# First attention: shared values weighed for two heads at a time, in three fp32r passes, with weight splits moved behind the own result

## The chip, the cores and the metric

One core of a Trainium2 chip runs the whole program. The metric is the device time of one execution in microseconds; lower is better. Five engines work side by side, each on its own instruction list in order, and wait for one another by semaphores: TensorE (PE in the profile, its weight loads PEld), VectorE (DVE), ScalarE (ACT), GpSimd (POOL), and SyncE (SP), which here issues DMAs.

## The reference

Two transformer layers of attention and feed-forward, with layer norms between; x is 4 x 256 tokens of 512. The change lies in the first attention only:

```python
q = (x @ w_q) ...            # 32 heads of 128
k = (x @ w_k) ...            # 8 heads
v = (x @ w_v) ...            # 8 heads, each shared by 4 query heads
lq = x @ w_lq                # 128 wide
lk = (lq @ w_lk) ...         # 32 heads of its own
lv = (x @ w_lv) ...          # 32 heads of its own
q, k, lk = rope(q), rope(k), rope(lk)
attn = causal_attn(q, repeat(k, 4), repeat(v, 4))
lat  = causal_attn(q, lk, lv)
return attn @ w_o + lat @ w_lo
```

So every query head is used twice: with the key and value shared by its group of four ("shared"), and with its own latent key and value ("own").

## The kernel before, in words

The first attention runs over 8 groups g of four heads (one shared key and value each). A group has 16 heads steps, 4 batches of 256 tokens by 4 heads h. A step s carries three heads at different stages, so the code speaks of `st` (this step), `before` (the step before, `st.near(-1)`) and `st.near(-2)`. The loop runs s from 2 to 17 in each group; h is s modulo 4, so steps 4, 8, 12 and 16 have h = 0. The steps at 16 and 17 already belong to the next group's first batch where there is one.

TensorE in a step (`a0_tensor_step`, L1074): `turn(0)`, three transposes of the normalised shared probabilities of `before` into bank PT; `scores()` of this head against shared and own keys, into banks 2 and 3; at h = 2 the keys of the next batch; `weigh(0)`, probabilities times shared values, into the first half of bank OB; `turn(1)` and later `weigh(1)`, the same for the own ones; the projection of the queries two steps ahead; `output(0)` and `output(1)`, the results of the head before the last times w_o and w_lo, added up in two banks over a batch; at h = 0 the values of the batch (`a0_values`). In step 16 TensorE waits, right before the values, for the weight chunks 6 to 10 (`weights(pe, st, range(C_LVV, C_WO))`).

Precision: nearly all products are made of fp32r parts. An operand is held as a high part (rounded by a ScalarE copy) and a low part (VectorE or GpSimd subtracts), and `product()` (L363 in the trace) makes three passes, high-high, high-low and low-high. Weighing and transposing were plain f32; there one matmul call shows as two MATMUL instructions in the trace.

ScalarE in a step (`a0_scalar_step`, L1210): copy of the turned shared probabilities (`turned_out(0)`, L1224), high part of the rotated queries (L1208), four exponentials (L1217), at h = 2 the key's swap, `result_hi(0)` (L1229), `turned_out(1)`, high parts of this step's weight chunks (L259), at h = 2 the key's high part, swap of the queries' halves (L1202, L1203), `result_hi(1)`.

VectorE (`a0_vector_step`, L1322): the rotation's sum of the queries (`a0_rotate`, L1319), minima of the scores (L1331, L1333), inverse sums, at h = 2 the key's sum, `result_lo(0)` (L1346), low parts of the weight chunks (L265), the cosine product (`a0_cosine`, L1310), `result_lo(1)`, at h = 1 the two additions to x (L1388), at h = 0 the values out of PSUM (L1353), and late splits. GpSimd does the sine product (L1417), the low part of the rotated queries (L1425) and the normalisation (L1436, L1438).

A group's weights are 19 chunks of 128 x 512: 0 keys, 1 to 4 queries, 5 latent keys, 6 to 10 values, 11 to 14 w_o, 15 to 18 w_lo. `SPLIT_AT` says in which step which chunks are split into W, `WEIGHTS_FOR` in which step TensorE waits for which. SyncE loads them into four raw buffers, each again as soon as its low part has been made.

## Time and profile before

| what | us |
|---|---|
| median of 3 runs | 1802.55 (1802.38 to 1802.89) |
| the profiled execution | 1804.75 |
| its span, first to last instruction | 1802.9 |
| TensorE busy | 1742.7 |
| VectorE, ScalarE, GpSimd busy | 1095.0, 1083.6, 931.1 |

Busy time counts any moment in which an engine has an instruction running. The span is what the views of the trace measure; what lies around it belongs to the launch. Ends of matmuls are modelled, so for TensorE the chain of work, which counts each matmul from the end of the one before, is the better measure of pace.

### The profile page before, as it was taken

What the parts mean: (1) busy time and instruction counts of PE and PEld (TensorE: products, weight loads), DVE (VectorE), ACT (ScalarE), POOL (GpSimd) and SP (SyncE); (2) the same over time, 40 slices, a digit from 0 to 9 for tenths busy, and PEclk for the clock granted to TensorE, in tenths of its full rate; (3) what the DMA queues carried; (4) which work ended last, traced back from release to release, by engine and by line L of the source; (5) the groups of instructions that cost most, each with busy time, mean ns of one, the idle gap of its engine ahead of it and who ended that gap; (6) DMA issues with size and microseconds to landing.
All of it is one profiled execution on the core that took longest, in us unless ns stands there. A gap on an engine that the chain in (4) does not pass through costs nothing.

```text
span 1802.9 us, 32176 instructions
## 1 busy us (share of the span) xinstructions
PE 1742.7 (97%) x11116; PEld 1520.7 (84%) x11116; DVE 1095.0 (61%) x3305; ACT 1083.6 (60%) x3077; POOL 931.1 (52%) x1170
## 2 busy tenths in 40 slices
PE   7999999999999999999999999999999998899798
PEld 6789999999999998999899899989888776677567
DVE  6675465556456546645654664565566677788756
ACT  3355566567556656655765664566563264788864
POOL 4555545455544555554555554455542255777850
PEclk9999999999999999999999999999999999999999
DMA  4300021012002101200110120020012121000101
GB/s 145 109 27 7 18 60 36 1 43 64 7 18 59 36 1 48 65 1 19 59 36 1 49 64 1 19 75 21 1 59 59 42 60 46 2 2 2 37 12 47
DMA packets 35424, 65.79 MB, mean 36 GB/s; under 512 B 4032, under 2 KB 4672, under 8 KB 35264
## 3 DMA queue, kind: packets, MB, share of 16 engines
q1 hardware_dynamic: 35264, 63.73, 11.7%
q8 instruction: 91, 1.49, 0.3%
q14 instruction: 69, 0.57, 0.1%
HBM read 61.62 MB, written 2.10 MB: 35 GB/s over the span
## 4 chain that ended last, share of the span: by engine, by line
PE 76%; DVE 8%; ACT 8%; issue 5%; POOL 3%; DMA 0%; SPq 0%; DVEq 0%; POOLq 0%; ACTq 0%
PE bank L363 58%; PE bank L1105 6%; PE bank L1092 4%; PE bank L1107 3%; ACT s L1217 2%; PE bank L1672 2%; PE bank L1643 1%; ACT s L1738 1%; DVE h L761 1%; PE bank L1659 1%; DVE work L772 1%; POOL h L839 1%; DVE work L1319 1%; ACT h L684 1%; POOL rstd L328 1%
## 5 line engine op out<-in xcount | busy, mean ns | idle before, releaser
L363 PE MATMUL bank<-W,oT 128*128 128x512 f32 x1632 | 432.2, 400 | 0.6 <-DVE x L1875 0.6
L1425 POOL TENSOR_TENSOR qk<-work,qk 128x512 fp32r<-128x512 f32 (+1 forms) x160 | 193.9, 1212 | 427.0 <-ACT qk L1208 427.0
L363 PEld LDWEIGHTS bank<-W,oT 128*128 128x128 f32 x1632 | 288.3, 189 | 48.5 <-DVE x L1875 1.1
L1224 ACT COPY pt<-bank 128x384 f32<-128x384 f32 x256 | 122.0, 477 | 324.0 <-PE bank L1092 323.3
L1417 POOL TENSOR_TENSOR work<-work,table 128x512 f32<-128x512 f32 (+1 forms) x160 | 190.8, 1192 | 132.8 <-ACT work L1203 132.8
L1217 ACT ACTIVATE s<-s,neg_max 128x128 f32<-128x128 f32 (+1 forms) x512 | 227.5, 445 | 49.1 <-DVE neg_max L1333 48.1
L363 PE MATMUL bank<-W,xnA 128*128 128x320 f32 (+1 forms) x1056 | 191.0, 335 | 2.3 <-DVE xnA L348 1.7
L1310 DVE TENSOR_TENSOR work<-bank,table 128x512 f32<-128x512 f32 (+1 forms) x160 | 102.1, 638 | 130.0 <-ACT work L1203 129.9
L363 PEld LDWEIGHTS bank<-W,xnA 128*128 128x128 f32 x1056 | 166.3, 189 | 15.2 <-DVE xnA L348 2.6
L1438 POOL TENSOR_TENSOR s<-s,inv_sum 128x256 f32<-128x256 f32 x256 | 168.2, 657 | 0.0
L363 PE MATMUL bank<-qk 128*128 128x256 f32 (+1 forms) x768 | 165.9, 351 | 0.9 <-POOL qk L1425 0.9
L1353 DVE COPY lvv<-bank 128x320 f32<-128x320 f32 x128 | 62.9, 491 | 169.6 <-PE bank L363 169.1
L363 PE MATMUL bank<-xnB,W 128*128 128x256 f32 (+1 forms) x1080 | 161.7, 299 | 0.9 <-DVE xnB L348 0.9
L1105 PE MATMUL bank<-pt,lvv 128*128 128x256 f32 x512 | 153.9, 382 | 8.9 <-DVE oT L1346 8.2
L363 PE MATMUL bank<-xnA,W 128*128 128x256 f32 (+1 forms) x1080 | 161.2, 299 | 0.6 <-DVEq L1264 0.3
L363 PEld LDWEIGHTS bank<-xnB,W 128*128 128x128 f32 x1080 | 143.2, 191 | 7.2 <-DVE xnB L348 1.3
L363 PEld LDWEIGHTS bank<-xnA,W 128*128 128x128 f32 x1080 | 143.1, 190 | 7.3 <-DVE work L1310 0.7
L1208 ACT CAST qk<-work 128x512 fp32r<-128x512 f32 (+1 forms) x160 | 92.4, 577 | 83.2 <-DVE work L1319 83.0
L1989 POOL TENSOR_TENSOR s<-s,b_inv_sum 128x384 f32<-128x384 f32 x128 | 114.1, 913 | 51.9 <-DVE b_inv_sum L1897 51.4
L265 DVE TENSOR_TENSOR W<-raw,W 128x512 fp32r<-128x512 f32 x148 | 108.2, 768 | 30.3 <-ACT W L259 30.1
L1436 POOL TENSOR_TENSOR s<-s,inv_sum 128x128 f32<-128x128 f32 x256 | 104.1, 407 | 42.0 <-DVE inv_sum L1341 42.0
L1092 PE MATMUL bank<-table,s 128*128 128x128 f32 x768 | 125.5, 272 | 0.0
(111 smaller groups left out, 3501.8 us busy)
## 6 DMA issues: line engine op xcount, KB each, us to landing
raw<-in_weights SPq DMA_DIRECT2D x215, 256.0 KB, 2.7
x<-in_x SPq DMA_DIRECT2D x8, 256.0 KB, 5.4
out<-x SPq DMA_DIRECT2D x8, 256.0 KB, 2.1
row<-in_bias_rows SPq DMA_DIRECT2D x5, 256.0 KB, 2.7
table<-in_constants SPq DMA_DIRECT2D x4, 240.0 KB, 3.1
b_qk<-in_bias_rows SPq DMA_DIRECT2D x1, 512.0 KB, 3.5
b_val<-in_bias_rows SPq DMA_DIRECT2D x1, 256.0 KB, 3.0
table<-in_constants SPq DMA_DIRECT2D x1, 66.0 KB, 2.4
```

What stands on the lines that cost most here:

```text
L265: nc.vector.tensor_tensor(dst[LO], raw[:, s, :], dst[HI].bitcast(F32), ALU.subtract).then_inc(w_split, 1)
L363: last = nc.tensor.matmul(out_ap, lhs(i), rhs(j), start=start and k == 0, stop=stop and k == 2)
L1092: last = nc.tensor.transpose(bank[PT][:, blk * P:(blk + 1) * P], s0[:, s, blk * P:(blk + 1) * P], ident)
L1105: nc.tensor.matmul(bank[OB][:, 0:SEQ], lvv[:, 0, col:col + P], pt0[:, k, 0:2 * P], start=True, stop=False)
L1217: last = nc.scalar.activation(s0[:, s, cols], s0[:, s, cols], ACT.Exp, bias=neg_max[:, s, qt:qt + 1], scale=-1.0, accum_out=row_sum[:, s, ...
L1224: nc.scalar.copy(pt0[:, k, :], bank[PT][:, 0:3 * P]).then_inc(a_pt, 1)
L1310: nc.vector.tensor_tensor(work[:, 2 + s, cols], bank[fs][:, cols], table[:, T_COS + cols.start:T_COS + cols.stop], ALU.mult).then_inc(a_pr ...
L1417: nc.gpsimd.tensor_tensor(work[:, s, cols], work[:, s, cols], table[:, T_SIN + cols.start:T_SIN + cols.stop], ALU.mult).then_inc(a_sin, 1)
L1425: nc.gpsimd.tensor_tensor(lo, work[:, 2 + s, st.columns(what)], hi.bitcast(F32), ALU.subtract).then_inc(a_rope_lo, 1)
L1436: nc.gpsimd.tensor_tensor(s0[:, s, 0:P], s0[:, s, 0:P], inv_sum[:, s, 0:1].to_broadcast([P, P]), ALU.mult)
L1438: nc.gpsimd.tensor_tensor(s0[:, s, P:3 * P], s0[:, s, P:3 * P], inv_sum[:, s, 1:2].to_broadcast([P, 2 * P]), ALU.mult).then_inc(a_norm, 1)
L1989: nc.gpsimd.tensor_tensor(blocks, blocks, b_inv_sum[:, at, 1:4].unsqueeze(2).to_broadcast([P, 3, P]), ALU.mult).then_inc(b_norm, 1)
```

## The change

The shared values get a high and a low part of their own (`vs`), and so do the turned shared probabilities (`pt_pair`, two heads side by side). ScalarE makes the high part of the probabilities as the first thing in a step (`turned_hi`), VectorE the low part as its first, ahead of the rotation's sum (`turned_lo`). In every even step `weigh_pair` weighs two heads' shared probabilities at once, in three fp32r passes, into the whole bank OB; its result is taken out by `pair_hi` and `pair_lo` on 512 columns. The own half stays f32, once a step (`weigh_own`). Both still share bank OB, and both turns bank PT: `turn(1)` now waits for the low part. `output(0)` comes one or two steps later than before: none at h = 2, one at h = 0 and h = 3, two at h = 1. ScalarE and VectorE make the parts of the weight chunks after the own result's part. Chunk 13 is split in step 3, chunk 12 in step 17; `WEIGHTS_FOR` follows.

```diff
 
-SPLIT_AT = {2: [17, 14], 3: [18], 11: [1], 12: [0, 2], 13: [3, 6], 14: [4, 7], 15: [8, 9],
-            16: [10, 11, 15, 12], 17: [16, 13]}
+SPLIT_AT = {2: [17, 14], 3: [18, 13], 11: [1], 12: [0, 2], 13: [3, 6], 14: [4, 7], 15: [8, 9],
+            16: [10, 11, 15], 17: [16, 12]}
 SPLIT_LATE = {13: [5]}
 SPLIT_FROM = 11
 TURN = [c for s in sorted(SPLIT_AT) for c in SPLIT_AT[s] + SPLIT_LATE.get(s, [])]
 OWN = sum(len(c) for s, c in SPLIT_AT.items() if s < SPLIT_FROM)
 BEFORE = TURN[OWN:]
 
-WEIGHTS_FOR = {2 + h: [C_WO + h, C_WLO + h] for h in range(GH)}
+WEIGHTS_FOR = {2: [C_WLO], 3: [C_WO, C_WLO + 1], 4: [C_WO + 1, C_WLO + 2],
+               5: [C_WO + 2, C_WO + 3, C_WLO + 3]}
 WEIGHTS_FOR.update({14: [C_K, C_Q], 15: [C_Q + 1], 16: [C_Q + 2], 17: [C_Q + 3]})
...
-                lvv = sb(s, "lvv", [P, 2, LVW])
-                pt0 = sb(s, "pt0", [P, 2, 3 * P])
-                oT0 = [sb(s, f"oT0_{i}", [P, 4, SEQ], F32R) for i in (HI, LO)]
+                lvv = sb(s, "lvv", [P, 2, GH * HD])
+                vs = [sb(s, f"vs{i}", [P, 2, HD], F32R) for i in (HI, LO)]
+                pt_pair = [sb(s, f"pt_pair{i}", [P, 2, 3, P], F32R) for i in (HI, LO)]
+                pt_own = sb(s, "pt_own", [P, 3 * P])
+                o_pair = [sb(s, f"o_pair{i}", [P, 2, SEQ], F32R) for i in (HI, LO)]
+                o_own = [sb(s, f"o_own{i}", [P, 2, SEQ], F32R) for i in (HI, LO)]
                 lqT = [sb(s, f"lqT{i}", [P, TOKENS], F32R) for i in (HI, LO)]
...
+            before = st.near(-1)
+
             def turn(k):
-                n, s = st.near(-1).inst(k)
+                n, s = before.inst(k)
                 pe.wait_ge(a_norm, n + 1)
-                pe.wait_ge(a_pt, n + 1)
+                if k == 0:
+                    pe.wait_ge(a_pt_own, before.number() + 1)
+                else:
+                    pe.wait_ge(a_pt_lo, before.number() + 1)
                 for blk in range(3):
                     last = nc.tensor.transpose(bank[PT][:, blk * P:(blk + 1) * P],
                                                s0[:, s, blk * P:(blk + 1) * P], ident)
                 last.then_inc(a_turned, 1)
 
-            def weigh(k):
-                before = st.near(-1)
-                n, _ = before.inst(k)
-                col = before.h * P if k else GH * P
-                if before.h == 0 and k == 0:
+            def weigh_pair():
+                pe.wait_ge(a_pt_lo, before.number() + 1)
+                pe.wait_ge(a_own_lo, before.number() + 1)
+                to = bank[OB][:, :].rearrange("p (e q) -> p e q", e=2)
+                product(to, lambda p: vs[p][:, 0, :],
+                        lambda p: pt_pair[p][:, :, 0:2, :].rearrange("p e b q -> p e (b q)"), True, False)
+                product(to[:, :, P:SEQ], lambda p: vs[p][:, 1, :],
+                        lambda p: pt_pair[p][:, :, 2, :], False, True).then_inc(a_pv_pair, 1)
+
+            def weigh_own():
+                col = before.h * P
+                if before.h == 0:
                     pe.wait_ge(a_proj_free, before.fill(3)[0] + 3)
-                pe.wait_ge(a_pt, n + 2)
-                pe.wait_ge(a_o_lo, n + 1)
-
-                nc.tensor.matmul(bank[OB][:, 0:SEQ], lvv[:, 0, col:col + P], pt0[:, k, 0:2 * P],
+                pe.wait_ge(a_pt_own, before.number() + 2)
+                if before.paired():
+                    pe.wait_ge(a_pair_lo, before.pair() + 1)
+                else:
+                    pe.wait_ge(a_own_lo, before.number() + 1)
+
+                nc.tensor.matmul(bank[OB][:, 0:SEQ], lvv[:, 0, col:col + P], pt_own[:, 0:2 * P],
                                  start=True, stop=False)
-                nc.tensor.matmul(bank[OB][:, P:SEQ], lvv[:, 1, col:col + P], pt0[:, k, 2 * P:3 * P],
-                                 start=False, stop=True).then_inc(a_pv, 1)
-
-            def output(k):
-                done = st.near(-2)
-                n, s = done.inst(k)
-                first, end = done.h == 0 and k == 0, done.h == GH - 1 and k == 1
+                nc.tensor.matmul(bank[OB][:, P:SEQ], lvv[:, 1, col:col + P], pt_own[:, 2 * P:3 * P],
+                                 start=False, stop=True).then_inc(a_pv_own, 1)
+
+            def output(k, done):
+                first, end = done.h == 0 and k == 1, done.h == GH - 1 and k == 1
                 if first:
                     pe.wait_ge(a_added, done.added)
                 if first and done.number() == 0:
                     pe.wait_ge(a_lq_lo, 2)
-                pe.wait_ge(a_o_lo, n + 2)
...
+                if k:
+                    pe.wait_ge(a_own_lo, done.number() + 2)
+                    of, slot = o_own, done.number() % 2
+                else:
+                    pe.wait_ge(a_pair_lo, done.pair() + 1)
+                    of, slot = o_pair, done.h % 2
                 w = ((C_WLO if k else C_WO) + done.h) * CH
                 for tt in range(2):
-                    last = product(bank[OUTB[tt]][:, :], lambda p: oT0[p][:, s, tt * P:(tt + 1) * P],
...
-            if lag1:
-                weigh(0)
+            if lag2 and st.h == 0:
+                output(0, st.near(-3))
+            if lag1 and before.paired():
+                weigh_pair()
                 turn(1)
             if st.queries and not st.first:
                 a0_queries(pe, st)
+            if lag1 and not before.paired():
+                turn(1)
...
-            if lag2:
-                output(0)
+            if lag2 and st.h in (1, 3):
+                output(0, st.near(-3))
+            if lag2 and st.h == 1:
+                output(0, st.near(-2))
+            if lag2 and st.h != 1:
+                output(1, st.near(-2))
             if lag1:
-                weigh(1)
-            if lag2:
-                output(1)
+                weigh_own()
+            if lag2 and st.h == 1:
+                output(1, st.near(-2))
             if st.h == 0 and st.heads:
                 if st.s == STEPS0:
                     weights(pe, st, range(C_LVV, C_WO))
...
             turn_of = None if st.last_group else st.g
             if lagging(st):
-                turned_out(0)
+                turned_hi()
             if before.queries:
                 a0_rope_hi(act, before, "q")
             if st.heads:
@@ -1239,19 +1295,20 @@
                 a0_swap(act, st, "k")
             if st.heads:
                 exponentials(1)
+            if lagging(st) and before.paired():
+                pair_hi()
             if lagging(st):
-                result_hi(0)
-                turned_out(1)
+                turned_own()
             if st.last_group and st.s == STEPS0:
                 first_use(ACT.Silu)
-            for stream, j, dst in step_splits(st, False):
-                stream.split_hi(act, j, dst, turn_of)
             if st.key:
                 a0_rope_hi(act, st, "k")
             if st.queries and not st.first:
                 a0_swap(act, st, "q")
             if lagging(st):
-                result_hi(1)
+                own_hi()
+            for stream, j, dst in step_splits(st, False):
+                stream.split_hi(act, j, dst, turn_of)
             for stream, j, dst in step_splits(st, True):
                 stream.split_hi(act, j, dst, turn_of)
             for t in next_norms(st):
...
+            def turned_lo():
+                dve.wait_ge(a_pt_hi, before.number() + 1)
+                hi, lo = [pt_pair[i][:, before.h % 2, :, :].rearrange("p b q -> p (b q)") for i in (HI, LO)]
+                nc.vector.tensor_tensor(lo, bank[PT][:, 0:3 * P], hi.bitcast(F32),
+                                        ALU.subtract).then_inc(a_pt_lo, 1)
+
+            def pair_lo():
+                dve.wait_ge(a_pair_hi, before.pair() + 1)
+                hi, lo = [o_pair[i][:, :, :].rearrange("p e q -> p (e q)") for i in (HI, LO)]
+                nc.vector.tensor_tensor(lo, bank[OB][:, :], hi.bitcast(F32),
+                                        ALU.subtract).then_inc(a_pair_lo, 1)
+
+            def own_lo():
+                dve.wait_ge(a_own_hi, before.number() + 1)
+                hi, lo = [o_own[i][:, before.number() % 2, :] for i in (HI, LO)]
+                nc.vector.tensor_tensor(lo, bank[OB][:, 0:SEQ], hi.bitcast(F32),
+                                        ALU.subtract).then_inc(a_own_lo, 1)
 
             def values(i):
                 tt, half = divmod(i, 2)
                 f, fs = st.fill(i)
                 dve.wait_ge(a_proj, f + 1)
-                nc.vector.tensor_copy(lvv[:, tt, half * HALF:(half + 1) * HALF],
-                                      bank[fs][:, 0:HALF]).then_inc(a_proj_free, 1)
+                if half == 0:
+                    nc.vector.tensor_copy(lvv[:, tt, 0:HALF], bank[fs][:, 0:HALF]).then_inc(a_proj_free, 1)
+                    return
+                own = GH * HD - HALF
+                shared = bank[fs][:, own:HALF]
+                nc.vector.tensor_copy(vs[HI][:, tt, :], shared).then_inc(a_v_hi, 1)
+                nc.vector.tensor_copy(lvv[:, tt, HALF:GH * HD], bank[fs][:, 0:own])
+                dve.wait_ge(a_v_hi, st.values_before() + tt + 1)
+                nc.vector.tensor_tensor(vs[LO][:, tt, :], shared, vs[HI][:, tt, :].bitcast(F32),
+                                        ALU.subtract).then_inc(a_proj_free, 1)
             turn_of = None if st.last_group else st.g
+            if lagging(st):
+                turned_lo()
             if before.queries:
                 a0_rotate(dve, before, "q")
             if st.heads:
@@ -1372,14 +1451,14 @@
                 ln_apply(dve, 16 + t, t % 2, x[:, t, :], normed[:, t, :])
             if st.key:
                 a0_rotate(dve, st, "k")
-            if lagging(st):
-                result_lo(0)
-            for stream, j, dst in step_splits(st, False):
-                stream.split_lo(dve, j, dst, turn_of)
+            if lagging(st) and before.paired():
+                pair_lo()
             if st.queries and not st.first:
                 a0_cosine(dve, st, "q")
             if lagging(st):
-                result_lo(1)
+                own_lo()
+            for stream, j, dst in step_splits(st, False):
+                stream.split_lo(dve, j, dst, turn_of)
             if st.h == 1 and not st.second:
                 done = st.near(-2)
                 for tt in range(2):
```

## Rows read from the trace of the kernel before

**Rows 1.** The page's busy line.

```profile
PE 1742.7 (97%) x11116; PEld 1520.7 (84%) x11116; DVE 1095.0 (61%) x3305; ACT 1083.6 (60%) x3077; POOL 931.1 (52%) x1170
```

**Rows 2.** Busy by window, from:to, length, engines, TensorE's granted clock, DMA.

```profile
230.00:250.00 20.00, 19.02 (x122) 16.88 (x121) 14.51 (x39) 14.32 (x39) 10.95 (x14) 1.00 0.20 58
1000.00:1200.00 200.00, 199.02 (x1266) 181.46 (x1265) 114.18 (x354) 126.27 (x356) 101.82 (x135) 1.00 0.13 38
```

**Rows 3.** The chain over a plain batch: start, length, what.

```profile
504.58 0.33 PE bank L1092 x3
504.91 1.06 PE bank L363 x6
505.97 0.43 PE bank L1105 x2
506.40 0.22 PE bank L1107 x2
...
506.95 3.18 PE bank L363 x21
...
510.79 1.39 PE bank L363 x6
...
512.51 2.48 PE bank L363 x18
...
535.00 8.42 PE bank L363 x54
543.42 0.33 PE bank L1092 x3
```

**Rows 4.** The chain, start of step 13 in the first and last group.

```profile
230.65 0.33 PE bank L1092 x3
...
1325.90 0.33 PE bank L1092 x3
```

**Rows 5.** Waits, 200 to 1280 us: total us, times, longest.

```profile
PE bank L1105 <- DVE oT L1346: 3.5, 7, 1.0
...
PEld bank L1105 <- ACT pt L1224: 9.5, 17, 1.4
```

**Rows 6.** The chain in steps 14 to 16.

```profile
558.23 0.67 PE bank L1105 x2
...
566.03 0.67 PE bank L1105 x2
...
574.51 8.42 PE bank L363 x54
```

**Rows 7.** ScalarE's timeline, steps 13 to 16: start, length of the instructions together.

```profile
550.70 0.62 ACT L259 CAST W<-raw 128x512 fp32r<-128x512 f32 x1
...
557.12 0.35 ACT L1229 CAST oT<-bank 128x256 fp32r<-128x256 f32 x1
557.37 0.48 ACT L1224 COPY pt<-bank 128x384 f32<-128x384 f32 x1
557.74 1.15 ACT L259 CAST W<-raw 128x512 fp32r<-128x512 f32 x2
...
559.22 0.58 ACT L1202 COPY work<-bank 64x512 f32<-64x512 f32 x1
...
565.34 0.47 ACT L1224 COPY pt<-bank 128x384 f32<-128x384 f32 x1
...
573.12 2.18 ACT L259 CAST W<-raw 128x512 fp32r<-128x512 f32 x4
```

**Rows 8.** VectorE's timeline, steps 13 and 14.

```profile
551.38 1.27 DVE L1388 TENSOR_TENSOR x<-x,bank 128x512 f32<-128x512 f32 x2
552.57 0.69 DVE L265 TENSOR_TENSOR W<-raw,W 128x512 fp32r<-128x512 f32 x1
553.17 0.69 DVE L1319 TENSOR_TENSOR work<-work 128x512 f32<-128x512 f32 x1
...
557.67 0.42 DVE L1346 TENSOR_TENSOR oT<-bank,oT 128x256 fp32r<-128x256 f32 x1
```

More of the change, by code:

```diff
@@ L901, in program @@
         a_turned = sem("a_turned")
-        a_pt = sem("a_pt")
-        a_pv = sem("a_pv")
-        a_o_hi = sem("a_o_hi")
-        a_o_lo = sem("a_o_lo")
+        a_v_hi = sem("a_v_hi")
+        a_pt_own = sem("a_pt_own")
+        a_pt_hi = sem("a_pt_hi")
+        a_pt_lo = sem("a_pt_lo")
+        a_pv_own = sem("a_pv_own")
+        a_pv_pair = sem("a_pv_pair")
+        a_own_hi = sem("a_own_hi")
+        a_own_lo = sem("a_own_lo")
+        a_pair_hi = sem("a_pair_hi")
+        a_pair_lo = sem("a_pair_lo")
         a_out = sem("a_out")
@@ L934, in near, with values_before, paired, pair @@
                 return Step(self.g, self.s + d)
+            def values_before(self):
+                return 2 * (self.g * BATCH + self.batch)
+            def paired(self):
+                return self.s % 2 == 1
+            def pair(self):
+                return self.number() // 2
             def number(self):
@@ L1117, in output @@
                     pe.wait_ge(a_lq_lo, 2)
-                pe.wait_ge(a_o_lo, n + 2)
+                if k:
[4 more added lines that the diff above has]
+                    of, slot = o_pair, done.h % 2
                 w = ((C_WLO if k else C_WO) + done.h) * CH
                 for tt in range(2):
-                    last = product(bank[OUTB[tt]][:, :], lambda p: oT0[p][:, s, tt * P:(tt + 1) * P],
+                    last = product(bank[OUTB[tt]][:, :], lambda p: of[p][:, slot, tt * P:(tt + 1) * P],
                                    lambda p: W[p][:, w:w + CH], first, end)
@@ L1260, in a0_vector @@
         def a0_vector(dve):
-            for s, n in ((a_proj_free, 2), (a_rope_lo, 2), (a_min, 2), (a_pt, 1), (a_o_lo, 1),
-                         (a_added, 1)):
+            for s, n in ((a_proj_free, 2), (a_rope_lo, 2), (a_min, 2), (a_pt_own, 1),
+                         (a_own_lo, 1), (a_added, 1)):
                 dve.sem_inc(s, n)
```

26 lines of the change are left out of this document (14 added, 12 removed).

## The prediction, made before the result was known

> **What bounds the kernel.** I read the busy line of the page first [rows 1]: TensorE is busy for 97% of the span, the others for 52 to 61%. Over 200 us in the middle of the first attention it is 99.5%, at full clock [rows 2]. So there TensorE's own order is the time, and what it saves comes back unless it then waits for somebody. The chain of work that ended last gives the true pace (it counts a matmul from the end of the one before), and a step can be added up from it [rows 3]: a turn (three transposes) 0.33 us; scores 1.06; one head's weighing 0.43 + 0.22 = 0.65; queries with one output 3.18, of which the output is 1.39, so queries 1.79; keys 2.48 - 1.06 = 1.42; values 8.42 - 1.39 = 7.03. A batch of four steps runs from 504.58 to 543.42, 38.84 us. Step 13 (numbers within a group) begins at 230.65 in the first group and at 1325.90 in the last [rows 4]: seven groups took 1095.25 us, where 28 plain batches would be 1087.5. So 7.7 us, 1.1 a group, are stalls. The table of waits says at what: at the weighing, for ScalarE's copy of the probabilities or for VectorE's low part [rows 5], and the chain shows them in steps 14 and 15, behind weight splits: pieces of 0.67 where 0.43 is usual [rows 6].
>
> **Gain on TensorE.** A pair of heads cost four weighings of 0.65 us. The two with own values stay. The two with the shared value head (1.30) become one product of three fp32r matmuls on 512 columns and three on 256. The scores have exactly these six, in strips of 256 and 128 columns: 1.06 us [rows 3]; elsewhere in the chain the same x6 piece reads 1.04 and 1.05. I take 1.05. Saved: 0.25 us a pair, 64 pairs, 16.0 us; 15 to 17 by the spread of the six. The outputs only move between steps, eight a batch as before. The steps' own lengths become 8.33 us (h=1, three outputs), 8.02 (h=2, one), 6.94 (h=3), 15.02 (h=0).
>
> The Trainium skill, "VectorE: DVE Perf Modes", section on the TRN2 errata, lists a matmul at max(60, 6 + columns) cycles, whatever its type. By it a head's f32 weighing of four instructions would be 0.33 us and the new product 0.98, so this edit would cost 0.32 us a pair, 20 us, instead of saving 16. The trace has 0.43 us for two f32 instructions of 256 columns [rows 3], where the rule gives 0.22, so the trace does not agree, and the row is taken.
>
> **Loss one: the values wait for chunk 10.** In step 16 (h=0) TensorE waits, just ahead of the values, for chunks 6 to 10, and chunk 10 is split in this very step. Before, ScalarE started those splits at 573.12 [rows 7], behind the copy of the probabilities, and the values began at 575.9 (574.51 plus an output) without a wait [rows 6]. Now the splits stand behind the own result, which exists only after the own weighing, TensorE's last instruction ahead of the values. Counted from its end: 0.03 to the result's copy, 0.25 until ScalarE can start the next (557.12 to 557.37), 0.62 for the split [rows 7], 0.03, 0.69 on VectorE, 0.38 until the matmul runs (VectorE's result ended at 558.09 [rows 8]; the weighing stretched by 0.24 from 558.23 ran as if from 558.47 [rows 6]). That is 2.0 us, with nothing to hide it, in seven groups (the last has no values to come): 14.0 us. Bounds: with no handover to TensorE 1.6 each, 11 us; with 0.2 more on VectorE and in the handovers 2.2 each, 15.4 us.
>
> **Loss two: VectorE comes late to the next step.** Call d the time from a step's start until VectorE takes up its first instruction, now the low part of the probabilities. On 384 columns, between 0.42 at 256 and 0.69 at 512 [rows 8], it takes 0.56, with 0.47 until the next starts. Queued behind it: the rotation's sum, so its high part on ScalarE, the minima, the exponentials, the own copy. In step 14 before, the sum started at 553.17 and the exponentials were done at 557.12, 3.95 later, keys between [rows 7, 8]. Now ScalarE's pair result follows (512 columns, 0.6 by its other casts of that size) and VectorE's low part of it (0.69). The own weighing shares their bank, so in an h=2 step it can go at d + 0.47 + 3.95 + 0.60 + 0.03 + 0.69 + 0.38 = d + 6.12; TensorE is there at 7.37. The pair's product can go at d + 0.56 + 0.42; TensorE is there at 2.81 (h=2) or 2.78 (h=0). In an h=3 step, with no keys (exponentials 0.9 earlier) and no pair, the own copy ends at d + 4.0 and is used 0.46 later (565.81 to 566.27 [rows 6, 7]); TensorE is there at 6.29.
>
> Without splits d is 0.8 to 0.95, and all of these hold, by 0.3 us or more: no stall. With them:
> Step 13 has two splits, the additions to x and a late split, now all behind the own result. From its start: weighing over at 6.95, VectorE's low part to 7.76, two low splits to 9.07, additions 1.19, late split 0.60 [rows 8]: 10.86, so d = 2.55 for step 14. Before it was 553.17 less 551.02 (543.42 plus 7.60), 2.15. Step 14 then stalls 0.72 at the pair and 0.62 more at the own weighing: 1.34, and lasts 9.36. ScalarE in it: own copy to 7.83, keys' high part to 8.2, swap of the queries 1.17 to 9.4 (two of [rows 7]'s 0.58), own result, two splits to 10.8; VectorE behind it to 11.6. So d = 2.25 in step 15: 0.42 at the own weighing. Its two splits leave d = 2.15 in step 16: 0.36 at the pair. Steps 17, 2 and 3 have two splits each too (3 had one before): d = 1.97 in step 2 gives 0.14 + 0.62, then 0.42 in step 3 and 0.36 in step 4. Sum 2.12 + 1.54 = 3.66 a group where 1.1 was, 2.56 more, in seven groups 17.9 us. In the last group steps 14 to 16 have no queries, so ScalarE and VectorE alone set them, and the new low parts lengthen their chain by 0.5 to 1 us each: 2 us. Bounds: with each of the six places 0.3 us milder, 5 us; 0.2 worse, 28 us. A gain is not excluded: the queries' cosine now comes ahead of the splits; if that healed the old stalls too, -7.7.
>
> **Hidden.** The shared values' high and low parts (three instructions in place of one copy of 320 columns) add 0.4 us on VectorE per half of tokens. TensorE fills a bank of values in 1.76 us, a quarter of 7.03, so this lies beside the values; only the last reaches into an h=1 step (d = 0.95), which has over 1 us to spare. Uncovered it would be 0.4 a batch, 13 us. ScalarE's pair copy replaces two of half its size. Chunks 12 and 13 are still split a step or more ahead of their outputs. Four raw buffers reload in about 3 us against a step's 7.
>
> **Sum.** -16.0 + 14.0 + 17.9 + 2 = +17.9 us. The profiled execution took 1804.75 us (its span 1802.9, and 1.85 around it), so it would be 1822.7; against the median of 1802.55, which is 2.2 lower, 1820.
>
> **Rivals.**
> A. Only chunk 10 counts; the slips are no worse than the old stalls. -16 + 14 = -2: 1800.5, within 0.2% (3.6 us, about what a measurement of this kernel can tell from no change). For it: the cosine no longer waits for splits. Against: VectorE was the releaser in step 14 even with d = 2.15, and now has more in front.
> B. The other side, faster: neither loss, only the shorter product. 1786.5; with half of loss one 1794. It is decided at one point: whether chunk 10's low part is ready within 0.6 us of the own weighing's end. For it: the pair's product is earlier than the old two weighings together. Against: own copy, split and low split cannot start before that weighing ends, and they are 1.3 us of work alone.
> C. The idle of 2 us costs TensorE its clock: values at 1.2 GHz, 7 us more in seven groups, 49 us: 1869. Against: between 230 and 250 us it idled 1 us in all, at clock 1.00 [rows 2]; no row shows 2 us in one piece. The Trainium skill, "TensorE: Matmul & The Clock Gate", section "Why this matters for your kernels", warns of idle gaps between bursts; the rows bear out only that shorter ones do no harm.
> D. The slips feed on each other: 5.5 us a group in place of 3.66, because steps 2 and 3 shrink and now have four splits. 1833.
>
> **Chances.** The forecast 0.60, D 0.12, C 0.03, A 0.13, B 0.12. So slower 0.75, same 0.12, faster 0.13. The likeliest is 1820, its own range 1808 to 1830; the range for 8 in 10 takes in A and half of B: 1794 to 1832.
>
> **What will show it.** Right: six-matmul pieces of about 1.05 us twice a batch in the chain and half as many f32 weighings; TensorE waits 2 us ahead of the values of every fourth batch, released by VectorE's split; steps 14 to 16 and 2 to 4 stall at the pair's product or the own weighing, behind VectorE or ScalarE. Wrong: values that begin without a wait, a d in step 14 of 2.15 or less, or plain batches that stall too. Their margin in h=2 is 0.3 us; if it is gone, 16 more steps pay, and it would be slower still.

## The result, and the profile after

The changed kernel takes 1842.48 us (1838.84 to 1844.56, four runs), the kernel before in the same session 1802.72: a ratio of 1.0214, 95% interval 1.0194 to 1.0235. It is slower, as forecast, but by 39.8 us where 17.5 were forecast, and outside the range of 1794 to 1832.

The page of the changed kernel, its busy line; TensorE is as busy as before, over a span 38.5 us longer (1841.4 against 1802.9):

```profile
PE 1743.9 (95%) x10988; PEld 1508.9 (82%) x10988; DVE 1159.0 (63%) x3498; ACT 1072.4 (58%) x3013; POOL 913.0 (50%) x1169
```

The chain of work that ended last, changed kernel, through steps 13 to 16 (start, length, what; step 17 starts at 595.64). L367 is `product()`, L1118 the turns, L1141 and L1143 the own weighing:

```profile
545.43 7.04 PE bank L367 x48
552.46 0.33 PE bank L1118 x3
552.79 2.84 PE bank L367 x21
555.63 0.33 PE bank L1118 x3
555.96 2.77 PE bank L367 x12
558.73 0.43 PE bank L1141 x2
559.16 0.23 PE bank L1143 x2
...
559.42 0.37 ACT o_own L1285
559.79 0.53 ACT W L263
...
560.35 1.29 DVE W L269 x2
561.64 0.16 DVE x L1467
...
588.33 7.31 PE bank L367 x48
595.64 0.33 PE bank L1118 x3
```

A batch without splits is TensorE's throughout. Here the chain leaves TensorE at the own result in step 13 and stays with ScalarE and VectorE for 21.7 us (559.42 to 581.12), until the pair's product of step 16. Before, it did so too in these steps, but for 13.2 us (544.86 to 558.10), until the weighing in step 14. From the start of step 13 (552.46) to that of step 17 (595.64) there are 43.18 us; a batch without splits lasts 38.22 (the values end at 514.25 and 552.46, a batch apart), where it was 38.84 [rows 3]. So a plain batch gains 0.62 us, and these four steps lose 4.96.

TensorE's timeline there; the brackets give its idle time and who ended it:

```profile
563.96 1.33 PE L367 MATMUL bank<-pt_pair,vs 128*128 128x512 f32 x6 [0.39 <-DVE pt_pair L1403]
...
569.63 0.67 PE L1141 MATMUL bank<-pt_own,lvv 128*128 128x256 f32 x2 [0.83 <-DVE o_pair L1409]
...
581.16 1.31 PE L367 MATMUL bank<-pt_pair,vs 128*128 128x512 f32 x6 [0.50 <-DVE pt_pair L1403]
...
588.33 1.88 PE L367 MATMUL bank<-W,xnA 128*128 128x320 f32 x11 [1.71 <-DVE W L269]
```

The forecast places are there: the pair's product in step 14, the own weighing in 14, the pair's product in 16, the values in 16; in step 15 the own weighing (576.97) runs 0.70 us instead of 0.59. The table of waits between 200 and 1300 us counts them over the groups (before: [rows 5]):

```profile
PE bank L367 <- DVE W L269: 11.9, 7, 1.7
PE bank L1141 <- DVE o_pair L1409: 11.7, 14, 0.8
PE bank L367 <- DVE pt_pair L1403: 10.1, 21, 0.5
```

Seven waits for chunk 10, 1.7 us each; with the slower start of the values behind (7.31 in place of 7.04) 1.96 each.

The whole difference, from starts of the same step in the two chains: step 5 of the first group comes 2.5 us later (155.55 against 153.07). From there seven groups take 1121.73 us against 1093.33, 28.4 more, or 160.25 against 156.19 a group. From step 5 of the last group to the layer norm's statistics that follow it in the chain (1399.16 against 1358.33) it is 121.9 us against 111.9, 10.0 more. After that the changed kernel is 2.3 us quicker. Sum 38.6.

The 2.5 us of the start hold slips of steps 2 to 4 (with fewer splits there, in e9, step 5 comes at 151.67) and a slow stretch of TensorE: behind an idle of 2.46 us (116.26 to 118.72) its granted clock was 0.52 between 120 and 122 us, and twelve output matmuls took 4.35 us in the chain where the kernel before took 2.76 at clock 1.00.

### The profile page after: what moved, and what is told of

Same layout as the page of the kernel before. It is cut to its first block, busy times and chain, and to the rows that moved or that the text cites. A ratio compares the mean times of both kernels' runs of the same rounds, so it can differ in the third digit from the quotient of the medians.

```text
span 1841.4 us, 32013 instructions
## 1 busy us (share of the span) xinstructions
PE 1743.9 (95%) x10988; PEld 1508.9 (82%) x10988; DVE 1159.0 (63%) x3498; ACT 1072.4 (58%) x3013; POOL 913.0 (50%) x1169
## 4 chain that ended last, share of the span: by engine, by line
PE 63%; DVE 13%; ACT 12%; issue 8%; POOL 3%; DMA 0%; DVEq 0%; SPq 0%; POOLq 0%; ACTq 0%
PE bank L367 51%; PE bank L1118 3%; DVE W L269 3%; ACT s L1264 3%; PE bank L1141 2%; DVE work L1376 2%; PE bank L1751 2%; ACT s L1817 1%; ACT work L1250 1%; ACT work L1249 1%; PE bank L1722 1%; DVE work L1367 1%; DVE pt_pair L1403 1%; DVE h L765 1%; PE bank L1143 1%
## 5 line engine op out<-in xcount | busy, mean ns | idle before, releaser
L1504 POOL TENSOR_TENSOR qk<-work,qk 128x512 fp32r<-128x512 f32 (+1 forms) x160 | 188.4, 1178 | 583.6 <-ACT qk L1255 583.5
L367 PE MATMUL bank<-W,xnA 128*128 128x320 f32 (+1 forms) x1056 | 193.0, 337 | 14.7 <-DVE W L269 11.9
L367 PE MATMUL bank<-W,o_own 128*128 128x512 f32 x768 | 202.4, 399 | 0.0
L1271 ACT CAST pt_pair<-bank 128x384 fp32r<-128x384 f32 x128 | 61.5, 480 | 238.1 <-PE bank L1118 238.1
L367 PE MATMUL bank<-W,o_pair 128*128 128x512 f32 x768 | 198.8, 401 | 0.0
L367 PEld LDWEIGHTS bank<-W,xnA 128*128 128x128 f32 x1056 | 165.5, 189 | 27.8 <-DVE W L269 13.3
L367 PE MATMUL bank<-qk 128*128 128x256 f32 (+1 forms) x768 | 166.0, 352 | 0.9 <-POOL qk L1504 0.9
L367 PEld LDWEIGHTS bank<-W,o_pair 128*128 128x128 f32 x768 | 140.2, 189 | 27.4
L367 PE MATMUL bank<-xnB,W 128*128 128x256 f32 (+1 forms) x1080 | 160.2, 298 | 0.8 <-DVE xnB L352 0.8
L1517 POOL TENSOR_TENSOR s<-s,inv_sum 128x256 f32<-128x256 f32 x256 | 160.4, 627 | 0.0
L367 PEld LDWEIGHTS bank<-W,o_own 128*128 128x128 f32 x768 | 139.5, 191 | 25.2
L367 PE MATMUL bank<-xnA,W 128*128 128x256 f32 (+1 forms) x1080 | 158.5, 297 | 0.6 <-DVEq L1321 0.3
L367 PEld LDWEIGHTS bank<-xnB,W 128*128 128x128 f32 x1080 | 146.4, 191 | 10.5 <-DVE xnB L352 1.3
L367 PEld LDWEIGHTS bank<-xnA,W 128*128 128x128 f32 x1080 | 145.4, 190 | 10.0 <-DVE work L1367 0.7
L1118 PE MATMUL bank<-table,s 128*128 128x128 f32 x768 | 126.6, 274 | 2.7 <-DVE pt_pair L1403 2.7
L1398 DVE RECIPROCAL inv_sum<-row_sum 128x2 f32<-128x2 f32 x256 | 42.1, 165 | 132.3 <-ACT s L1264 132.3
L367 PE MATMUL bank<-W,xnB 128*128 128x320 f32 x768 | 116.5, 311 | 0.0
```

What stands on the lines that cost most here:

```text
L367: last = nc.tensor.matmul(out_ap, lhs(i), rhs(j), start=start and k == 0, stop=stop and k == 2)
L1118: last = nc.tensor.transpose(bank[PT][:, blk * P:(blk + 1) * P], s0[:, s, blk * P:(blk + 1) * P], ident)
L1271: nc.scalar.copy(pt_pair[HI][:, before.h % 2, :, :].rearrange("p b q -> p (b q)"), bank[PT][:, 0:3 * P]).then_inc(a_pt_hi, 1)
L1398: nc.vector.reciprocal(inv_sum[:, s, :], row_sum[:, s, :]).then_inc(a_inv, 1)
L1504: nc.gpsimd.tensor_tensor(lo, work[:, 2 + s, st.columns(what)], hi.bitcast(F32), ALU.subtract).then_inc(a_rope_lo, 1)
L1517: nc.gpsimd.tensor_tensor(s0[:, s, P:3 * P], s0[:, s, P:3 * P], inv_sum[:, s, 1:2].to_broadcast([P, 2 * P]), ALU.mult).then_inc(a_norm, 1)
```

## Experiments

Each is compared with the kernel before in the same session, which took 1803.9 to 1805.4 us there. "Group" is the mean time from step 5 of one group to step 5 of the next, over seven groups. "Early" and "late" say where a step splits its weight chunks: ahead of the own result, as before, or behind it, as in the change.

| kernel | us | ratio, 95% interval | group, us |
|---|---|---|---|
| before | 1802.7 | 1 | 156.19 |
| changed | 1842.5 | 1.0214 (1.0194 to 1.0235) | 160.25 |
| e1 changed, splits early | 1791.7 | 0.9927 (0.9911 to 0.9944) | 154.42 |
| e2 changed, early in step 16 only | 1833.6 | 1.0159 (1.0144 to 1.0175) | 158.67 |
| e3 changed, sum ahead of low part | 1853.9 | 1.0276 (1.0260 to 1.0291) | 161.67 |
| e5 before, splits late | 1819.0 | 1.0081 (1.0066 to 1.0096) | 158.10 |
| e4 as e1, sum ahead of low part | 1810.4 | 1.0027 (1.0016 to 1.0038) | 156.70 |
| e6 changed, no low part | 1809.0 | 1.0027 (1.0016 to 1.0038) | 156.99 |
| e7 changed, ScalarE early, VectorE late | 1900.1 | 1.0523 (1.0507 to 1.0538) | 167.83 |
| e8 as e1, splits spread | 1791.8 | 0.9923 (0.9908 to 0.9938) | 154.28 |
| e9 changed, splits spread | 1835.5 | 1.0167 (1.0150 to 1.0184) | 159.25 |
| e10 before, late, one VectorE instruction more | 1851.4 | 1.0258 (1.0243 to 1.0274) | 161.99 |
| e11 before, one VectorE instruction more | 1828.7 | 1.0138 (1.0123 to 1.0153) | 158.93 |
| e12 changed, old step lengths | 1866.5 | 1.0353 (1.0337 to 1.0368) | 164.10 |
| e13 as e1, old step lengths | 1835.3 | 1.0178 (1.0161 to 1.0195) | 160.17 |

### e1: the splits back at their old place

First ScalarE's step, then VectorE's:

```diff
             if st.last_group and st.s == STEPS0:
                 first_use(ACT.Silu)
+            for stream, j, dst in step_splits(st, False):
+                stream.split_hi(act, j, dst, turn_of)
...
             if lagging(st):
                 own_hi()
-            for stream, j, dst in step_splits(st, False):
-                stream.split_hi(act, j, dst, turn_of)
...
             if lagging(st) and before.paired():
                 pair_lo()
+            for stream, j, dst in step_splits(st, False):
+                stream.split_lo(dve, j, dst, turn_of)
...
             if lagging(st):
                 own_lo()
-            for stream, j, dst in step_splits(st, False):
-                stream.split_lo(dve, j, dst, turn_of)
```

> The changed kernel with the weight splits back at their old place on both engines (ScalarE behind the own probabilities' copy, VectorE behind the pair's low part); all else as changed. Theory S, the loss is the splits' place: the wait for chunk 10 (2.0 us a group, 14 us) goes, and most of the slips in steps 14 to 16 and 2 to 4 (5.3 us a group now): 1792 to 1802 us. Rival L, the loss is the longer chain of the pair itself (a low part at the head of VectorE's queue, a 512-column result): only the 14 us go, 1828.

1791.7 us: the edit of place alone is worth 50.8 us, and with the splits in their old place the rest of the change makes the kernel 0.7% faster than before. That is Theory S's side and not Rival L's. It does not yet say why the place costs so much; e5 shows that the place alone does not. Of the 50.8 us, 40.8 lie in the seven groups and the rest mostly in the last one.

### e2: early in step 16 only

ScalarE's step (VectorE's in the same way, with `pair_lo`, `own_lo` and `split_lo`):

```diff
                 first_use(ACT.Silu)
+            if st.s == STEPS0:
+                for stream, j, dst in step_splits(st, False):
+                    stream.split_hi(act, j, dst, turn_of)
             if st.key:
...
                 own_hi()
-            for stream, j, dst in step_splits(st, False):
-                stream.split_hi(act, j, dst, turn_of)
+            if st.s != STEPS0:
+                for stream, j, dst in step_splits(st, False):
+                    stream.split_hi(act, j, dst, turn_of)
```

> The changed kernel with the splits at their old place in step 16 alone. Both theories: the wait ahead of the values goes, 7 x 2.0 = 14 us, so 1828 us; a little less if step 17 inherits nothing. If that wait only took up lateness that would show somewhere else, the time stays at 1842.

1833.6 us, 8.9 less, where 14 were expected. The wait ahead of the values costs 1.96 us a group, but only 1.58 us a group came back, and from step 5 of the last group to the end it is 3.0 us longer than in the changed kernel (567.1 against 564.1). Why is open.

### e3 and e4: the rotation's sum ahead of the low part

```diff
-            if lagging(st):
-                turned_lo()
             if before.queries:
                 a0_rotate(dve, before, "q")
+            if lagging(st):
+                turned_lo()
```

> The changed kernel with VectorE's low part of the probabilities behind the rotation's sum instead of ahead of it; splits stay late. Rival L: exponentials come 0.5 us earlier in every late step, so six places a group gain up to 0.5: about 20 us less, 1822. Theory S: the own weighing gains, but the pair's product waits 0.6 us longer for the low part where it already stalls; 1836 to 1842.

> Splits early as in the first experiment, and VectorE's low part of the probabilities behind the rotation's sum. If the head of VectorE's queue is what the late steps pay for, up to 0.5 us in three or four places a group: 1778 to 1787. If, as with the late splits, the pair's product then waits for its low part in the late steps and nothing else is gained: 1791 to 1800.

Late splits: 1853.9, 11 us worse. Early splits: 1810.4, 19 us worse. Both lie outside all that was expected. My expectation for rival L was badly reasoned: the exponentials wait for the minima, which stand behind both instructions in either order, so nothing comes sooner for them; only the low part, and with it the pair's product, comes later. The change's own place for the low part is the better one, by 11 to 19 us.

### e5: late splits in the kernel before

The two loops stand behind `result_hi(1)` and `result_lo(1)`:

```diff
-            for stream, j, dst in step_splits(st, False):
-                stream.split_hi(act, j, dst, turn_of)
...
                 result_hi(1)
+            for stream, j, dst in step_splits(st, False):
+                stream.split_hi(act, j, dst, turn_of)
...
                 result_lo(0)
-            for stream, j, dst in step_splits(st, False):
-                stream.split_lo(dve, j, dst, turn_of)
...
                 result_lo(1)
+            for stream, j, dst in step_splits(st, False):
+                stream.split_lo(dve, j, dst, turn_of)
```

> The kernel before with one edit, the splits behind the own result on both engines, no pair and no low part. Theory S: the wait for chunk 10 adds 14 us and the slips 2 to 3 us a group, 1830 to 1838. Rival L: only the wait, 1817.

1819.0: the wait for chunk 10 (1.91 us a group, 13.4 in seven) and little else. The same late splits cost 14.5 us here and 50.8 in the changed kernel. So neither theory was enough: the slips come from the splits' place and the rest of the change together.

### e6: no low part

```diff
-            if lagging(st):
-                turned_lo()
...
-                               bank[PT][:, 0:3 * P]).then_inc(a_pt_hi, 1)
+                               bank[PT][:, 0:3 * P]).then_inc(a_pt_lo, 1)
...
-                        lambda p: pt_pair[p][:, :, 0:2, :].rearrange("p e b q -> p e (b q)"), True, False)
+                        lambda p: pt_pair[HI][:, :, 0:2, :].rearrange("p e b q -> p e (b q)"), True, False)
...
-                        lambda p: pt_pair[p][:, :, 2, :], False, True).then_inc(a_pv_pair, 1)
+                        lambda p: pt_pair[HI][:, :, 2, :], False, True).then_inc(a_pv_pair, 1)
```

> The changed kernel (splits late) without the low part of the probabilities: VectorE's subtraction is left out, and the pair's product repeats the high part in its place, so TensorE has the same six matmuls. If the late splits hurt because this kernel's chain of VectorE and ScalarE is longer by that 0.5 us a step, five late steps a group gain 0.5 to 0.9 each: 1812 to 1822. If the chain's length does not matter and the shorter h=2 and h=3 steps do, at most the pair's waits go: 1832 to 1840.

1809.0, below both expectations: one VectorE instruction of 0.55 us per step, 128 in all, with the handover that waits for it, is worth 33.5 us of the 39.8, with late splits. That is half of its whole busy time. In the seven groups it is 22.8 us; 9.7 more lie behind step 5 of the last group.

### e7: ScalarE early, VectorE late

VectorE's step as in the changed kernel; ScalarE's:

```diff
                 first_use(ACT.Silu)
+            for stream, j, dst in step_splits(st, False):
+                stream.split_hi(act, j, dst, turn_of)
...
                 own_hi()
-            for stream, j, dst in step_splits(st, False):
-                stream.split_hi(act, j, dst, turn_of)
```

> ScalarE's high parts of the chunks back at their old place, VectorE's low parts still behind the own result. If it is ScalarE's queue that carries the lateness on, this returns most of the 50 us: 1795 to 1808. If VectorE's, only the split's 0.6 us drops out of the wait ahead of the values (4 us) and a little of each slip: 1825 to 1835.

Neither expectation: 1900.1, far worse than both late (1842.5) and both early (1791.7). This is what led to the explanation below. Its trace shows something else too. First TensorE's timeline:

```profile
597.84 1.32 PE L367 MATMUL bank<-pt_pair,vs 128*128 128x512 f32 x6 [1.57 <-DVE pt_pair L1403]
606.39 5.97 PE L367 MATMUL bank<-W,xnA 128*128 128x320 f32 x21 [3.07 <-DVE W L269]
```

Then the windows around that wait (from:to, length, busy by engine, TensorE's granted clock third from the end):

```profile
560.00:600.00 40.00, 35.99 (x224) 31.74 (x223) 25.44 (x77) 22.06 (x62) 17.20 (x22) 1.00 0.18 60
600.00:606.00 6.00, 3.32 (x21) 2.81 (x19) 2.54 (x6) 4.78 (x12) 3.54 (x6) 0.97 0.01 1
606.00:611.00 5.00, 4.61 (x17) 4.61 (x18) 2.03 (x4) 0.00 (x0) 0.00 (x0) 0.50 0.40 105
611.00:616.50 5.50, 5.50 (x36) 5.49 (x35) 1.28 (x5) 0.00 (x0) 0.00 (x0) 0.87 0.01 3
```

After an idle of 3.07 us the values started at clock 0.50, the 1.2 GHz level, and took 10.03 us in the chain instead of 7.04. That group is the worst; in the other six the same values took 8.6 to 8.9 us. Against the 7.31 of the changed kernel the clock costs e7 1.6 us a group.

### e8 and e9: splits spread

```diff
-SPLIT_AT = {2: [17, 14], 3: [18, 13], 11: [1], 12: [0, 2], 13: [3, 6], 14: [4, 7], 15: [8, 9],
+SPLIT_AT = {2: [17], 3: [18], 4: [14, 13], 11: [1, 0], 12: [2], 13: [3, 6], 14: [4, 7], 15: [8, 9],
             16: [10, 11, 15], 17: [16, 12]}
```

> Splits early, and spread: one each in steps 2 and 3, chunks 14 and 13 in the long step 4, chunk 0 in step 11. Steps 2 to 4 lose their stalls, about 0.5 us a group: 1785 to 1789. If those steps had no stall left: 1791 as in the first experiment.

> The changed kernel with splits still behind the own result, but only one each in steps 2 and 3, chunks 14 and 13 in the long step 4, and chunk 0 in step 11; steps 13 to 17 have what they had. Ring theory (in a late step ScalarE and VectorE form one closed chain of 7.60 us for h=3 and 9.60 for h=2 with two splits, against 6.94 and 8.02 of TensorE): a split fewer shortens it by 0.7, so steps 2 to 4 lose most of their 2.4 us a group, steps 14 to 16 keep theirs: 1826 to 1832. If the order alone hurts, whatever the number of splits: 1838 to 1842.

With early splits nothing measurable, 1791.8, so the 0.5 us a group of the expectation was not there to gain (the start is 2.3 us quicker in the trace, a group 0.14, the medians are equal). With late splits 1835.5, 7 us less, where 10 to 16 were expected: from step 17 to step 5 a group takes 39.4 us where it was 40.6 (nominal 38.2), so the stall there halves, but step 11 with its second chunk adds 0.3.

### e10 and e11: one VectorE instruction more in the kernel before

The extra instruction reads the table and writes a tile that nothing uses; in e10 the splits are late as in e5.

```diff
+            if lagging(st):
+                dve.wait_ge(a_pt, before.inst(0)[0] + 2)
+                nc.vector.tensor_tensor(extra[:, :], table[:, T_COS:T_COS + 3 * P],
+                                        table[:, T_SIN:T_SIN + 3 * P], ALU.subtract)
             if before.queries:
                 a0_rotate(dve, before, "q")
```

> The kernel before with late splits (1819) and one instruction more: at the head of VectorE's step, after the copy of the probabilities, a 384-column subtraction whose result nobody uses. Its outputs stay where they were, so TensorE's steps keep 9.02 and 7.59 us. Ring theory: the ring grows from 7.41 to 7.9 (h=3) and from 9.14 to 9.6 (h=2), now longer than TensorE's steps, so the slips come in: 2 to 3.5 us a group, 1833 to 1844. If the shorter h=2 and h=3 steps of the changed kernel are what matters: 1819 to 1824.

> The kernel before, splits where they were, with the same extra instruction: the control. Ring theory: the ring with early splits has less to carry but is close to TensorE's steps already, so it costs less than with late splits: 0.3 to 1 us a group, 1807 to 1812. If the extra instruction costs the same with early and late splits, this one rises as much over 1804 as the other over 1819.

1851.4 and 1828.7. The direction is as the ring theory says, the sizes are not: the instruction costs 32 us with late splits, where at most 25 were expected, and 24 with early ones, where at most 8 were. The kernel before was already close to the point where its ScalarE and VectorE bind, with early splits too; in a batch without splits the instruction costs next to nothing (38.97 us against 38.84). Late splits then cost 22.8 us, against 14.5 without it: so the longer ring explains only 8 of the 36 us by which late splits cost more in the changed kernel.

### e12 and e13: the old step lengths

Nine idle transposes (0.33 us for three) behind the own weighing at h=2, six at h=3:

```diff
+            if lag1 and st.heads and st.h in (2, 3):
+                for i in range({2: 9, 3: 6}[st.h]):
+                    nc.tensor.transpose(bank[PT][:, i % 3 * P:(i % 3 + 1) * P], ident, ident)
```

> The changed kernel with nine idle transposes (0.33 us for three) after the own weighing at h=2 and six at h=3, so these steps are as long as in the kernel before. Uncovered they cost 1.66 us a batch, 53 us. If the shorter steps are why lateness is carried on, ScalarE and VectorE catch up in them: 20 to 25 us come back, 1868 to 1876. If step length does not matter: 1890 to 1898.

> The same idle transposes with the splits at their old place (1792 without them). The stalls left there, 1.5 us a group and 2 in the last, come back: about 10, so 1832 to 1838. If step length does not matter: 1845. The difference to the late one then says what late splits cost at the old step lengths: 30 to 40 us by the first reading, 50 by the second.

1866.5 and 1835.3, the first 1.5 us below its expectation, the second as expected: the late splits now cost 31.2 us instead of 50.8. The padding, 53 us if uncovered, costs 24 with late splits and 43.6 with early ones. So 20 of the 51 us hang on the two short steps, 13 of them in the seven groups.

## Why the prediction was off

**Gain on TensorE.** Right, a little undersized: 0.62 us a plain batch, 19.8 us over 32 batches, against 16.0. The x24 piece of scores, keys and pair's product lasts 3.53 us, the sum of my rows, so the product costs what I took for it. The rest of the gain is spread: the steps from 514.25 to 552.47 last 8.30, 8.04, 6.91 and 14.96 us against my 8.33, 8.02, 6.94 and 15.02. By the cycle rule of the Trainium skill's "VectorE: DVE Perf Modes", section on the TRN2 errata, which I set aside, the edit would have cost 20 us, an estimate from that page's figure. The plain batch got shorter, so the trace does not agree: what the f32 weighings cost is the row's 0.43 us [rows 3]. (The page's row names no type; "whatever its type" was my reading of that.)

**Loss one.** Right: 1.96 us in seven groups, 13.7 us against 14.0, with the chain as forecast, own result, its high part, the split's high part, its low part.

**Loss two is the step that failed.** The places were right, the size was not. Without the wait for chunk 10, stalls are 160.25 - 152.88 (four batches of 38.22) - 1.96 = 5.41 us a group, against 3.66 forecast, and 0.83 before over the same groups, where I had 1.1 (my window took in a stall of the last group). That is 32.1 us in seven groups instead of 17.9, and above my bound of 28. That bound was added up wrongly too: six places 0.2 us worse make 26.3. Step 14 begins at 560.77 (step 13 is not stalled until its last output), and from there:

| step | forecast | measured |
|---|---|---|
| 14 | 1.34 | 1.73 |
| 15 | 0.42 | 0.43 |
| 16, ahead of the values | 0.36 | 0.80 |
| 17 and 2 to 4 | 1.54 | 2.40 |

(The last row is 636.26 - 595.64 - 38.22.) One term was missing and one too small. The missing one is the key's rotation sum. In an h=2 step it stands on VectorE between the exponentials and the pair's low part, and the sum that gave d + 6.12 has no term for it. VectorE's timeline of the changed kernel in steps 14 and 15:

```profile
568.33 0.55 DVE L1376 TENSOR_TENSOR work<-work 128x256 f32<-128x256 f32 x1 [0.27 <-issue]
568.81 0.68 DVE L1409 TENSOR_TENSOR o_pair<-bank,o_pair 128x512 fp32r<-128x512 f32 x1
...
571.48 1.55 DVE L269 TENSOR_TENSOR W<-raw,W 128x512 fp32r<-128x512 f32 x2
572.96 0.55 DVE L1403 TENSOR_TENSOR pt_pair<-bank,pt_pair 128x384 fp32r<-128x384 f32 x1
...
578.75 0.41 DVE L1415 TENSOR_TENSOR o_own<-bank,o_own 128x256 fp32r<-128x256 f32 x1
579.08 1.55 DVE L269 TENSOR_TENSOR W<-raw,W 128x512 fp32r<-128x512 f32 x2
580.56 0.54 DVE L1403 TENSOR_TENSOR pt_pair<-bank,pt_pair 128x384 fp32r<-128x384 f32 x1
```

ScalarE's half of the pair's result was done at 568.33, but VectorE took up the other half at 568.81, behind the key's sum. From the measured d my terms give 560.77 + 2.59 + 0.47 + 3.95 + 0.60 + 0.03 = 568.41. The 0.40 us between are the whole excess of step 14, 1.73 against 1.34. The key's high part on ScalarE waits for the same sum, so the swap of the queries ended at 9.75 instead of 9.4. The term that was too small is the low splits: two of them take 1.48 us until the next instruction, where I had 1.31, and VectorE was done 0.99 us behind ScalarE's last cast instead of 0.8.

The forecast d = 2.55 for step 14 came out at 563.36 - 560.77 = 2.59, but instead of 2.25 and 2.15 in steps 15 and 16 it was 2.44 and 2.67. It did not decay.

**The mechanism** is one that I had in pieces. In a late step ScalarE and VectorE are one closed ring, as the chain above shows between 559.42 and 581.12: low part, rotation's sum, exponentials (at h=2 with the key's swap, sum and high part), own copy, swap of the queries, cosine, own low part, splits, and the next step's low part. The ring's length is the time from one rotation's sum to the next. What it exceeds TensorE's step by is either waited for or carried into the next step. The sums' starts on VectorE, changed kernel (L1376):

```profile
563.83 0.68 DVE L1376 TENSOR_TENSOR work<-work 128x512 f32<-128x512 f32 x1
...
573.43 0.68 DVE L1376 TENSOR_TENSOR work<-work 128x512 f32<-128x512 f32 x1
...
581.03 0.68 DVE L1376 TENSOR_TENSOR work<-work 128x512 f32<-128x512 f32 x1
```

and the kernel before with late splits, e5 (L1319):

```profile
557.07 0.68 DVE L1319 TENSOR_TENSOR work<-work 128x512 f32<-128x512 f32 x1
...
566.20 0.68 DVE L1319 TENSOR_TENSOR work<-work 128x512 f32<-128x512 f32 x1
...
573.62 0.68 DVE L1319 TENSOR_TENSOR work<-work 128x512 f32<-128x512 f32 x1
```

Read in the same way in each trace, steps 14 and 15 (two splits each). "Late" is the time from TensorE's first turn of step 14 to the rotation's sum in it, "excess" the two rings less TensorE's two steps:

| kernel | late | ring h=2, h=3 | TensorE h=2, h=3 | excess | stalls a group |
|---|---|---|---|---|---|
| before | 2.34 | 8.85, 7.42 | 9.02, 7.59 | -0.3 | 0.8 |
| e5 before, late | 2.78 | 9.13, 7.42 | 9.02, 7.59 | -0.1 | 0.8 |
| e11 early, one more | 3.13 | 9.16, 7.72 | 9.02, 7.59 | 0.3 | 3.6 |
| e10 late, one more | 3.57 | 9.60, 7.88 | 9.02, 7.59 | 0.9 | 4.7 |
| e1 changed, early | 2.18 | 8.90, 7.17 | 8.02, 6.94 | 1.1 | 1.5 |
| e13 early, padded | 2.18 | 9.03, 7.57 | 9.02, 7.60 | 0.0 | 0.8 |
| e12 late, padded | 3.22 | 9.59, 7.64 | 9.02, 7.60 | 0.6 | 2.7 |
| changed | 3.22 | 9.60, 7.60 | 8.02, 6.94 | 2.2 | 5.4 |
| e7 | 3.66 | 10.37, 8.65 | 8.02, 6.94 | 4.1 | 13.0 |

(Stalls without 1.96 for chunk 10 where splits are late; e7's hold the 1.6 of its slow clock.) The excess is no independent cause: in the changed kernel it is the stalls of the two steps and the growth of d, 1.73 + 0.43 + 0.08. What shows the cause is the chain, which does not touch TensorE there, and the runs that alter one length at a time: e6 and e10 the ring, e12 the steps.

The change did both things at once: it lengthened the ring, by the low part, and moved an output out of h=2 (9.02 to 8.02 with the pair's product in it) and one head's shared weighing, 0.65 us, out of h=3. With early splits, ScalarE's high parts are in the ring, while VectorE makes the low ones beside ScalarE's swap. With late splits it is VectorE's low ones, while the high ones run beside the cosine and the own low part. In e7 both are in it, hence 1900.

The excess alone does not order the kernels: e11 pays 3.6 us with 0.3, e1 only 1.5 with 1.1. How late the ring stands when step 14 begins counts as well, 3.13 us in e11 and 2.18 in e1. In e11 the own weighing of step 14 waits 1.53 us in one piece, and steps 15 and 16 have no wait. Late splits act on both: they lengthen step 13's tail on VectorE (2.18 in e1, 3.22 in the changed kernel), and they lengthen the ring behind it.

What stays open: at the old step lengths late splits cost 31 us in the changed kernel, and 23 in the old one with a VectorE instruction of the low part's length. The 8 us between may be the pair's result of 512 columns ahead of the own copy; that was not tried alone and is not shown.

**The last group** cost 10.0 us, with the gain of the product in it, where I had 2 for the chain. TensorE's waits there, and the windows (granted clock third from the end):

```profile
1368.28 1.39 PE L367 MATMUL bank<-pt_pair,vs 128*128 128x512 f32 x6 [1.82 <-DVE pt_pair L1403]
...
1378.53 0.52 PE L1118 MATMUL bank<-table,s 128*128 128x128 f32 x3 [2.69 <-DVE pt_pair L1403]
...
1388.89 1.50 PE L367 MATMUL bank<-pt_pair,vs 128*128 128x512 f32 x6 [2.26 <-DVE pt_pair L1403]
```

```profile
1370.00:1372.00 2.00, 2.00 (x11) 2.00 (x10) 0.56 (x3) 2.00 (x8) 2.00 (x4) 0.50 0.01 3
1374.00:1376.00 2.00, 1.84 (x13) 1.34 (x11) 1.00 (x2) 1.50 (x4) 0.00 (x0) 1.00 0.00 0
1390.00:1400.00 10.00, 10.00 (x42) 8.35 (x42) 4.47 (x8) 3.97 (x7) 0.00 (x0) 0.84 0.16 54
```

Without queries the ring of these steps goes through TensorE. From 1374.5 to 1378.53 the chain is: the own weighing's end, ScalarE's high part of its result, a split's high part, two low splits, a normed tile's low parts, the low part of the probabilities, and then TensorE. The idle is followed by a lower clock: the output pieces from 1372.01, 1380.10 and 1391.04 last 1.80, 4.17 and 2.46 us in the chain, together 2.9 more than the 1.39, 2.77 and 1.39 of a plain batch. With early splits (e1) the same group costs 2.0 us more than before and runs at clock 1.00 between 1340 and 1400.

**Rivals.** A and B: no; a wait and the slips were both there. D, slips that feed on each other, is what happened in kind; it gave 5.5 us a group, and 5.4 was measured. That it hit the size is in part luck: it named only steps 2 and 3, and steps 14 to 16 grew as much (2.96 against 2.12). It missed the last group and the start, so that its 1833 is still 9 us short. C, the clock: not at the wait for chunk 10, where 1.7 us of idle left the clock at 1.00 (588 to 596 us); but at the start, in the last group, and in e7 in the main groups. "TensorE: Matmul & The Clock Gate" of the Trainium skill, section "Why this matters for your kernels", warns of idle between bursts; these traces agree, e7 with clock 0.50 behind 3.07 us.

**The version to keep** is e1, 1791.7 us: the paired product in three passes with the low part ahead of the rotation's sum, and the splits ahead of the own result.

## What to carry to other kernels

Where two engines hand a step's work back and forth and neither is busy above 65%, measure their ring: the time from one instruction to the same one a step later, in a late step. Compare it with the bound engine's own step, step by step and not as a mean; a batch that fits as a whole can have two steps that do not. Look also at how late the ring already stands when the short steps begin. Before an edit that moves filler work behind a result, look at who waits for the filler, and whether its engine's partner can do its half beside something else.

## What was not expected of the hardware

- TensorE's clock fell to the 1.2 GHz level behind waits in a busy stretch: 0.50 between 606 and 611 us in e7 behind 3.07 us (and 1.57 us eight us earlier), 0.52 between 120 and 122 in the changed kernel behind 2.46 us, 0.50 between 1370 and 1372 in the same kernel behind 1.82 us. Behind the wait of 1.71 us for chunk 10 it stayed at 1.00 (588 to 596 us). What else decides between the last two is not shown.
- Two low splits on VectorE took 1.48 us to the next instruction wherever they began beside GpSimd's sine product (571.48, 579.08), and 1.21 us where they did not (560.35). Whether the sine product is the reason was not tried alone.
